# Projected tokens kept in one on-chip tensor across two programs of a kernel

## The reference

```python
v = h @ p_w + p_b                                  # per pixel: 3 features to 32 channels
for i in range(4):
    v = fourier_layer(v, W1, W2) + einsum("bcxy,cd->bdxy", v, w_w[i]) + w_b[i]
    v = batchnorm(v) * bn_g[i] + bn_b[i]
    if i < 3: v = relu(v)
h = squeeze(einsum("bcxy,cu->bxyu", v, q_w) + q_b) # projected pixels: (32, 64, 64)
for i in range(4):                                 # attention, tokens of 64 numbers
    x = x + linear_attn(layernorm(x), Wq, Wk, Wv, Wo, bo)
    x = x + gelu(layernorm(x) @ W1 + b1) @ W2 + b2
h = layernorm(h + x)
h = layernorm(h + mixture_of_experts(h))
```

## Time and profile before

| | |
|---|---|
| median of 3 timed runs | 816.8 us |
| the three runs | 800.74, 816.8, 819.63 us |
| the profiled execution | 800.96 us |
| its span in the trace | 799.2 us |
| mean granted TensorE clock | 0.918 |
| TensorE matmul busy | 645.6 us (81%) |
| VectorE busy | 554.3 us (69%) |
| ScalarE busy | 359.9 us (45%) |
| GpSimd busy | 51.1 us (6%) |

### The profile page before, as it was taken

How to read it: one execution, slowest core, us unless ns; L and a number is a source line. 1 busy time by engine, 2 the same in 40 slices (tenths; PEclk the granted TensorE clock), 3 DMA queues, 4 the chain that set the end, 5 groups by cost and what they waited for, 6 DMA issues and landing times. The chain is left out here.

```text
span 799.2 us, 22402 instructions
## 1 busy us (share of the span) xinstructions
PE 645.6 (81%) x10251; PEld 435.9 (55%) x10251; DVE 554.3 (69%) x802; ACT 359.9 (45%) x485; POOL 51.1 (6%) x88
## 2 busy tenths in 40 slices
PE   3889946676899736758899389999968989998997
PEld 2866732235767512338676134335447878787844
DVE  7859868993398869954688778836218675747463
ACT  0034559400145578000355588635014747474662
POOL 4100000003000000021000000020001111020200
PEclk9989986998699959995999689999979999999998
DMA  8400000006000000051000000040050000000001
GB/s 319 101 2 3 2 1 1 2 1 240 2 2 2 2 0 2 1 186 55 2 2 2 0 2 3 2 159 23 16 190 1 2 1 1 1 2 1 1 1 28
DMA packets 12271, 27.29 MB, mean 34 GB/s; under 512 B 3472, under 2 KB 4368, under 8 KB 12176
## 3 DMA queue, kind: packets, MB, share of 16 engines
q1 hardware_dynamic: 11888, 25.12, 9.2%
q10 hardware_dynamic: 288, 0.73, 0.3%
HBM read 24.80 MB, written 1.05 MB: 32 GB/s over the span
## 5 line engine op out<-in xcount | busy, mean ns | idle before, releaser
L444 ACT ACTIVATE V<-ps,wts 128x1024 f32<-128x1024 f32 x96 | 101.8, 1111 | 249.0 <-PE ps L791 249.0
L618 DVE BATCH_NORM_STATS2 stats<-V 128x6 f32<-128x512 f32 x192 | 117.9, 676 | 16.0 <-ACT V L444 16.0
L494 DVE STREAM_TRANSPOSE A<-V 128x2048 f32<-128x2048 f32 x48 | 107.3, 2275 | 6.7 <-ACT V L393 6.7
L393 ACT ACTIVATE V<-V,small 128x2048 f32<-128x2048 f32 x48 | 96.7, 2082 | 4.9 <-DVE small L646 4.9
L690 PE MATMUL ps<-A,tab 128*128 128x384 f32 x192 | 71.9, 512 | 30.9 <-DVE A L501 30.9
L678 PE MATMUL ps<-A,tab 32*32 32x512 f32 x1536 | 67.0, 644 | 25.4 <-DVE A L494 25.4
L612 DVE STREAM_TRANSPOSE A<-ps 128x2048 f32<-128x2048 f32 x24 | 55.4, 2315 | 34.3 <-PE ps L776 34.3
L690 PEld LDWEIGHTS ps<-A,tab 128*128 128x128 f32 x192 | 34.5, 193 | 78.8 <-DVE A L501 57.2
L791 PEld LDWEIGHTS ps<-tab,A 64*128 64x128 f32 x1024 | 62.4, 195 | 27.3 <-issue 27.3
L501 DVE STREAM_TRANSPOSE A<-ps 128x1024 f32<-128x1024 f32 x48 | 56.7, 1221 | 19.1 <-PE ps L678 19.1
L791 PE MATMUL ps<-tab,A 64*128 64x128 f32 x1024 | 68.5, 286 | 0.0
(11 more groups left out here) (233 smaller groups left out, 909.4 us busy)
## 6 DMA issues: line engine op xcount, KB each, us to landing
A<-in_modes SPq DMA_DIRECT2D x32, 384.0 KB, 6.7
r_ky<-in_modes SPq DMA_DIRECT2D x16, 384.0 KB, 6.5
wl<-in_layers SPq DMA_DIRECT2D x3, 452.0 KB, 5.9
wm<-in_mixture SPq DMA_DIRECT2D x1, 874.5 KB, 8.2
tab<-in_table SPq DMA_DIRECT2D x1, 656.5 KB, 4.8
A<-in_turned SPq DMA_DIRECT2D x1, 512.0 KB, 3.6
V<-in_pixels SPq DMA_DIRECT2D x4, 128.0 KB
tower_out<-A SPq DMA_DIRECT2D x2, 256.0 KB, 2.2
```

The lines of the kernel that those rows point to most:

```text
L393: nc.scalar.activation(pair, pair, ACT.Relu, bias=bias, scale=scale).then_inc(s_relu, 1)
L444: nc.scalar.activation(Vm[:, 2 * h:2 * h + 2, r, 512 * q:512 * (q + 1)], bank(half_of_u(q, r) + 2 * h, 2).rearrange("p (m n) -> p m n", m= ...
L494: nc.vector.transpose(T[n % 3].rearrange("p (k n) -> p k n", k=16), Vk[:, :, P * n:P * (n + 1)]).then_inc(s_T, 1)
L618: last = nc.vector.bn_stats(stats[:, 16 * q + 4 * r + m, :], Vm[:, m, r, 512 * q:512 * (q + 1)])
```

## The change

The tower's room becomes a tensor named `room` that outlives the tower. The token program takes it over, reads the projected pixels `u0` in it where the tower wrote them, and lays six of its own tensors (`u0T`, `xT`, `sqT`, `h0T`, `hT`, `qs`) into the rest. `u_out` moves to its first 1024 columns; `z_one` and `g_one` move behind. The table `natural` and a second copy of `centre` (`first_centre`) leave `cst` or are added, and are loaded by SyncE into columns 1024 to 1279 once the last mode mixing is done. The store of the pixels and the four loads of tokens are gone, and so are the waits on them. TensorE's wait for `cst` moves behind the first two groups of matmuls. The functions not shown are as before.

```diff
-    return table, np.concatenate([grid, last_tables(freq)], axis=1), spectra.reshape(P, 3 * MODES)
+    return table, np.concatenate([grid, last_tables(freq), token_constants()[:, NATURAL:], token_constants()[:, 2 * P:3 * P]], axis=1), spectra.reshape(P, 3 * MODES)
...
+KEPT_TOKENS, KEPT_TABLE, KEPT_ALL = 0, 1024, 1280
+ROOM = 8192
+shared = ExitStack()
+rooms = []
...
+        A = shared.enter_context(nc.sbuf_tensor("room", [P, ROOM], f32))
+        rooms.append(A)
-        A = sb("A", [P, 8192])
...
-        z_one, g_one, u_out = A[:, 0:768], A[:, 1024:2048], A[:, 2048:3072]
+        z_one, g_one = A[:, 2048:2816], A[:, 3072:4096]
+        u_out, kept_table = A[:, KEPT_TOKENS:KEPT_TABLE], A[:, KEPT_TABLE:KEPT_ALL]
...
-            sp.dma_start(last_t[:, 0:L_TURNED], grid[:, GRID_ALL:]).then_inc(s_last, 16)
+            sp.dma_start(last_t[:, 0:L_TURNED], grid[:, GRID_ALL:GRID_ALL + L_TURNED]).then_inc(s_last, 16)
             sp.dma_start(last_t[:, L_TURNED:], weights[:, W_TURNED:]).then_inc(s_last, 16)
-            rows = tower_out.rearrange("a (r n) -> (a r) n", r=8)
-            for h, done in enumerate((s_ua, s_uv)):
-                sp.wait_ge(done, 1)
-                sp.dma_start(rows[:, 512 * h:512 * (h + 1)], u_out[:, 512 * h:512 * (h + 1)]).then_inc(s_out, 16)
-            sp.wait_ge(s_out, 32)
+            sp.wait_ge(s_mix, KYP * L)
+            sp.dma_start(kept_table, grid[:, GRID_ALL + L_TURNED:]).then_inc(s_out, 16)
+            sp.wait_ge(s_out, 16)
+            sp.wait_ge(s_ua, 1)
+            sp.wait_ge(s_uv, 1)
...
+NATURAL = 3 * P + 2 + EXPERTS
...
-        u0 = sb("u0", [P, NX])
-        u0T = sb("u0T", [P, NX])
...
+        ctx.callback(shared.close)
+        kept = rooms.pop()
+
+        def in_room(i):
+            return kept[:, KEPT_ALL + NX * i:KEPT_ALL + NX * (i + 1)]
+
+        u0T = in_room(0)
...
-        cst = sb("cst", [P, 4 * P + 2 + EXPERTS])
+        cst = sb("cst", [P, NATURAL])
...
-        natural = cst[:, 3 * P + 2 + EXPERTS:]
+        u0, natural, first_centre = (kept[:, a:b] for a, b in ((KEPT_TOKENS, KEPT_TABLE), (KEPT_TABLE, KEPT_TABLE + P),
+                                                               (KEPT_TABLE + P, KEPT_ALL)))
...
-            for g in range(G):
-                rows = tower_out.rearrange("a (r n) -> (a r) n", r=8)
-                sp.dma_start(part(u0, g), rows[:, GW * g:GW * (g + 1)]).then_inc(s_u[g], 16)
             for l in range(1, DEPTH):
...
-            nc.scalar.dma_start(cst[:, :], table).then_inc(s_cst, 16)
+            nc.scalar.dma_start(cst[:, :], table[:, 0:NATURAL]).then_inc(s_cst, 16)
...
-            pe.wait_ge(s_cst, 16)
             for g in range(G):
-                pe.wait_ge(s_u[g], 16)
                 for t in range(GP):
                     last = nc.tensor.matmul(bank(g, 0, P * t, P), part(u0, g)[:, P * t:P * (t + 1)], natural, start=True, stop=True)
                 last.then_inc(s_utr, 1)
             for g in range(G):
                 pe.wait_ge(s_uraw, g + 1)
-                nc.tensor.matmul(bank(g, 1), centre, part(h0T, g), start=True, stop=True).then_inc(s_ucen, 1)
+                nc.tensor.matmul(bank(g, 1), first_centre, part(h0T, g), start=True, stop=True).then_inc(s_ucen, 1)
+
+            pe.wait_ge(s_cst, 16)
```

More of the change, by code:

```diff
@@ L998, in sem @@
             return ctx.enter_context(nc.semaphore(name))
-        u0 = sb("u0", [P, NX])
-        u0T = sb("u0T", [P, NX])
[L1002 to L1006, removed]
+        ctx.callback(shared.close)
[3 more added lines that the diff above has]
+        u0T = in_room(0)
+        xT = in_room(1)
+        sqT = in_room(2)
+        h0T = in_room(3)
+        hT = in_room(4)
+        qs = in_room(5)
         qe = sb("qe", [P, NX])
@@ L1042, in stat @@
             return st[:, i, GT * g:GT * (g + 1)]
-        s_u = [sem(f"s_tokens{g}") for g in range(GROUPS)]
         s_wl = [sem(f"s_wl{l}") for l in range(DEPTH)]
```

## The result

| | before | changed |
|---|---|---|
| timed runs | 20 | 20 |
| median | 803.38 us | 797.25 us |
| lowest to highest | 796.66 to 819.63 us | 793.14 to 810.05 us |
| ratio, changed to before | | 0.9952, 95% interval 0.9929 to 0.9974 |
| profiled execution | 800.96 us | 807.52 us |

The changed kernel is faster by 0.48% (0.26 to 0.71%): 3.9 us of the 801 us that the comparable runs of the kernel before took, 2.1 to 5.7 us with the interval. That is under the 2% line.

What follows compares the result with a forecast made beforehand. The prediction took the join, where every engine stood still from 585.69 to 591.43 except for transfers, and half-clock matmuls behind it, as the bound. Earlier restart and matmul times gave 6.6 us: 800.96 - 6.6 = 794.4 us, range 790 to 814.

Steps and rivals of the forecast that it cites:

- The mechanism's sum: At the join of tower and token program: copies of `u0T` end 6.6 us earlier, taken as the whole gain.
- the offset: Whole run: timed runs may lie an unexplained 16 to 19 us higher, with either kernel.
- Part 1, the barrier: End of tower: store and its wait go, barrier stays; loads issued about 586.05 instead of 588.09, 2.04 us earlier.
- Part 2, the tables: Table load near 557 costs nothing, with 28 us of cover; TensorE restarts 5.28 us earlier in the token program.
- Part 3, the clock at the join: First token matmuls: clock falls at 586.8, returns at 590.2; `u0T` copies end at 591.9 to 592.0, gain 6.6 us.
- The other ends: First token matmuls: no clock fall, `cst` decides, gain 7.4 us; or clock low from restart for 5.5 us, gain 5.3.
- Part 4, the loads: Token program's other loads: smaller `cst` priced at nothing; layer 0's weights need 4.7 to 5.9 us, arriving in time.
- The late arrival: Rival, token program's start: late `cst` or layer 0 weights replace the removed wait; gain 2.6 us, 798.3 us, chance 0.12.
- signs of being wrong: In the trace: barrier gap over 1 us, instruction block there, VectorE or GpSimd waiting for loads, larger shift elsewhere.
- The fetch of instructions: Rival, token program's start: TensorE waits for its instructions; 3.3 us slower, 804.3 us; chance of net loss 0.05.
- the time stays within 2%: Whole run: changed kernel's time differs from the kernel before by less than 2%, 16 us; chance 0.78.
- The 0.18 for faster by over 2%: Whole run: over 2% faster only if old kernel reads at its upper, new at its lower level; chance 0.18.

Runs made afterwards that it cites:

- e4: The kernel before, repeated word for word; ratio to the kernel before 1.0018 (0.9986 to 1.0050).
- e8: The changed kernel plus one idle matmul in the last layer, ahead of the mode mixing; ratio to the kernel before 0.9940 (0.9911 to 0.9969).
- e10: The kernel before plus only the idle matmul ahead of the mode mixing; ratio 0.9968 (0.9947 to 0.9989), all 12 runs from 798.5 to 802.5 us.
- e11: The changed kernel plus three idle matmuls ahead of TensorE's wait for `cst`, which stays late; ratio to the kernel before 0.9888 (0.9855 to 0.9921).
- e3: Half of the change: tables fetched ahead, pixels still sent through memory as in the kernel before; ratio to that kernel 1.0015 (0.9990 to 1.0039).
- e2: Half of the change: tokens kept on chip, tables loaded with `cst` as in the kernel before; ratio to that kernel 0.9998 (0.9958 to 1.0038).
- e5: The changed kernel, repeated word for word; ratio to the kernel before 0.9961 (0.9925 to 0.9996).
- e1: The changed kernel with `cst` loaded early, in the tower, into the shared tensor, without waits for it; ratio to the kernel before 0.9931 (0.9894 to 0.9969).

## Why the prediction was right and where it was wrong

**The time, 794.4 us, and what it stood against: wrong.** The mechanism's sum was 6.6 us, 0.8%. But it was taken from the profiled execution at 800.96 us, and so 794.4 stood 22.4 us below the median of 816.8 us then shown. The step that failed is the offset: "No row tells what the 16 to 19 us are, so I keep them as an offset that either kernel may carry." The rows held a hint, the 3.4 us at half clock at 535.6 in the earlier trace rows, which I used only as a pattern for the join. What the runs showed in place of an unexplained offset is that same stretch: in long runs it lasts 38 us and costs some 13 us (`e4`), with the idle matmul ahead of it no long run came (`e8`, `e10`), and it is no level that a kernel carries. With 20 runs the kernel before has a median of 803.38 us, so 13 of the 22.4 us were an accident of three runs, two of them long. The measured distance was 6.1 us between medians and 3.9 by the ratio. The wide range, 790 to 814, did hold 797.25.

**Part 1, the barrier: right.** The writer ended at 599.02 and the loads were issued at 599.51, 0.49 us later; I had 0.39. VectorE's drain ended together with it, at 599.1:

```profile
L209 DVEq DRAIN  x1: 764/764/764, 598.3 to 598.3; - x1
L209 SPq COMPARE_BRANCH  x1: 33/33/33, 599.1 to 599.1; - x1
```

**Part 2, the tables: right.** The table load was issued at 569.27, behind the last mixing, and landed 2.1 us later, 28 us ahead of its use. TensorE started 0.5 us behind the writer in place of 5.8, a gain of 5.2 us in the first pair of traces (forecast 5.28).

**Part 3, the clock at the join: wrong in place, nearly right in sum.** I had it fall at the barrier and cost the first matmuls. In no trace of the changed join did it. L1483 and L1487 ran at full clock, the first of the cases under "The other ends", and `cst` decided, as that case says. The copies ended 6.1 to 6.2 us behind the writer; the forecast was 6.3. Two errors cancelled there, so the agreement is luck: the clock that did not fall, and a `cst` later than priced.

**What followed the copies: the term that was missing.** The sum stopped at the copies and took the rest as unchanged. The clock fell 7.9 to 8.7 us behind the writer, set off by the idle time in the wait for `cst`, and 1.6 us went back (`e11`). That brings 7.1 us at the copies down to 5.2 at the reduction. The interval of the ratio, 2.1 to 5.7 us, holds 5.2 and not 6.6. But the reduction is not the end. Up to VectorE's last write the traces gain 6.4 us in the mean, because two of the three changed ones have one later stretch of 3.4 us at half clock where each of the kernel before has two. The third, `e8`, has three and gains 4.5 to 5.3. Such stretches come and go between executions, and the runs' median time at half clock is the same in both kernels. So the missing term is shown at the join, and why the runs gain 3.9 us where the traces gain 4.5 to 7.6 stays open.

**Part 4, the loads: mis-sized.** "which I price at nothing" set the smaller size against the larger neighbour and left `cst` at 3.3 us; it took 4.1 to 4.3, and 2.4 where SyncE's loads came behind it. Beside the loads of tokens it had been 3.3 and 3.5, and 3.2 in `e3`, which keeps those loads. The neighbour was the cost and the size was not: without the four loads of 128 KB ahead of the large ones it took longer at either size (`e2`). The weights of layer 0 took 6.3 and 6.5 us instead of my 4.7 to 5.9, and still came in time.

**The rivals.** The late arrival is what happened in kind. I had it decide beyond a landing of `cst` at 590.3; on that scale, 4.8 us behind the writer, it landed at 590.5, with 1.6 us of clock behind it. One of my own signs of being wrong came with it, VectorE waiting for `cst` past L1487, and another, a stretch elsewhere that moved by more than the join gained: the mixing in the profiled execution, which the change does not touch. The fetch of instructions did not occur. In 597 to 603 the changed kernel's rows have the two data queues alone:

```profile
q1 hardware_dynamic: 144, 0.48, 27.4%
q10 hardware_dynamic: 117, 0.17, 10.3%
```

That the time stays within 2% had the chance 0.78 and was right. The 0.18 for faster by over 2% was a chance of being misled by levels, and 20 runs removed it.

## What to carry to other kernels

When a wait has two arrivals behind it, taking one away gives little, and so does the other; cost the pair, and then ask what comes next in line and what its new neighbours on the queues are. Order loads by first use even across queues: one wait on SyncE gave 3.2 us at the join here, about half of it transfer and half clock. Follow the sum to an event behind the next possible fall of the clock, and, before using a profiled execution as the base, explain why the timed runs differ from it.

## What the runs showed of the hardware

An idle time of 1.4 to 1.5 us on TensorE can cost more later than where it lies: the granted clock fell to half 2.0 us behind one such hole (the kernel before, 533.6) and 2.1 to 3.0 us behind another (the changed kernel, `e5`, `e8`), while TensorE was busy. It does not always fall: in `e1` and `e3` it stayed at full behind the first hole.

A half-clock stretch did not always end when TensorE was busy again. In the mode mixing with its many small matmuls, ten traces without the idle matmul had none (two), one of 3.4 us (one), of 14 to 17 us (three) or of 38 to 41 us (four), the longest with TensorE counted busy throughout. None occurred in the four traces with one idle matmul of 1.1 us ahead of it. Over 34 and 20 runs one microsecond at half clock went with 0.36 us of the kernel's time.

A 195 KB load took 2.4 and 2.5 us with only one later load on its own queue beside it, and 4.1 to 4.3 us beside four loads of another queue. That queue's first load was issued at the same moment.
